# A fused gated-scan and FFN layer on eight cores: one of two calls of a LayerNorm phase is taken out of the block loop

## What is computed

```python
x = x + attn(layernorm(x))      # layer A
x = x + ffn(layernorm(x))       # layer B
# attn: h = rmsnorm(x); q,k,v,g = h @ wq, h @ wk, h @ wv, h @ wg
#       a = sigmoid(h @ wa); y_t = a_t * y_(t-1) + k_t * v_t   (scan over tokens)
#       return (q * y * silu(g)) @ wo
# ffn:  xr, xk = blends of x and x shifted by one token (mu_r, mu_k)
#       return sigmoid(xr @ W_r.T) * (square(relu(xk @ W_k.T)) @ W_v.T)
```

## Time and profile before

| | us |
|---|---|
| median of 2 runs (lowest, highest) | 871.05 (869.91, 872.19) |
| the profiled execution, own time | 864.63 |
| its span on the slowest core, core 4 | 863.1 |
| spans of all cores | 834.6 to 863.1 |
| PE, DVE, ACT busy on core 4 | 622.9, 350.2, 275.0 |

### The profile page before, as it was taken

One profiled execution on the slowest core, in us unless ns is written; L12 is line 12 of the kernel. 1 busy time (PEld: TensorE's weight loads), 2 busy tenths in 40 slices (PEclk: granted clock), 3 DMA queues, 4 the chain that ended last, 5 costly groups with the idle time before them and its releaser, 6 DMA issues.

```text
span 863.1 us, 12981 instructions; the slowest of 8 cores (834.6 to 863.1 us)
## 1 busy us (share of the span) xinstructions
PE 622.9 (72%) x4864; PEld 522.8 (61%) x4864; DVE 350.2 (41%) x656; ACT 275.0 (32%) x432; POOL 5.1 (1%) x13
## 2 busy tenths in 40 slices
PE   0000008799789799959896999799979697998085
PEld 0000006687678588948795888587858596877064
DVE  0002702323824374437343833383437443834222
ACT  2000003126233614462346134523361435232321
POOL 2000000000000000000000000000000000000000
PEclk9999999988778788979997888788879898888577
DMA  8999992001100410141014101410041003001101
GB/s 168 186 186 165 172 160 37 1 1 26 25 1 12 124 38 1 42 107 26 1 50 102 22 2 49 98 25 1 15 121 38 1 18 82 1 2 49 24 1 49
DMA packets 52876, 48.10 MB, mean 56 GB/s; under 512 B 47440, under 2 KB 47568, under 8 KB 51664
## 3 DMA queue, kind: packets, MB, share of 16 engines
q1 hardware_dynamic: 51520, 28.40, 13.2%
q0 software_dynamic: 1296, 18.87, 13.1%
HBM read 46.22 MB, written 8.39 MB: 63 GB/s over the span
## 4 chain that ended last, share of the span: by engine, by line
PE 53%; DVE 17%; DMA 13%; another core or an unknown queue 7%; ACT 4%; issue 4%; DVEq 1%; SPq 0%; ACTq 0%; POOLq 0%
PE pp L194 50%; DMA xhat_fm<-stg 8%; DVE fC L404 5%; DVE xh_fm L484 3%; PE pp L209 3%; DMA W_wk<-wk 3%; DMA out<-x_tm 2%; DVE y2b L474 2%; DVE fB L395 2%; DMA xh_fm<-bfP 1%; DVE fC L469 1%; DVE x_tm L224 1%; ACT bfP L455 1%; ACT bfP L247 1%
## 5 line engine op out<-in xcount | busy, mean ns | idle before, releaser
L194 PE MATMUL pp<-xhat_fm,W_wk 128*128 128x256 bf16 x512 | 74.7, 321 | 175.3 <-DMA xhat_fm<-stg 175.3
L194 PEld LDWEIGHTS pp<-xhat_fm,W_wk 128*128 128x128 bf16 x512 | 57.9, 114 | 191.3 <-issue 176.6
L194 PE MATMUL pp<-y2b,W_wrT 128*128 128x256 bf16 x512 | 68.8, 305 | 29.9 <-DVE y2b L474 27.4
L194 PE MATMUL pp<-xh_fm,W_wkT 128*128 128x256 bf16 x512 | 71.1, 312 | 19.1 <-DVE fC L414 19.1
L194 PEld LDWEIGHTS pp<-y2b,W_wrT 128*128 128x128 bf16 x512 | 55.5, 109 | 42.1 <-issue 30.5
L194 PEld LDWEIGHTS pp<-xh_fm,W_wkT 128*128 128x128 bf16 x512 | 56.4, 111 | 33.6 <-issue 21.1
L194 PE MATMUL pp<-xhat_fm,W_wg 128*128 128x256 bf16 x512 | 64.7, 294 | 4.4 <-DVE fC L414 4.4
L194 PE MATMUL pp<-xh_fm,W_wvT 128*128 128x256 bf16 x512 | 65.6, 296 | 3.0 <-ACT xh_fm L504 3.0
L194 PE MATMUL pp<-xhat_fm,W_wq 128*128 128x256 bf16 x512 | 64.3, 293 | 1.8 <-ACT fB L386 1.8
L194 PE MATMUL pp<-xhat_fm,W_wv 128*128 128x256 bf16 x512 | 64.3, 293 | 0.0
L194 PE MATMUL pp<-y2b,W_wo 128*128 128x256 bf16 x512 | 64.3, 293 | 0.0
(11 more groups left out here) (64 smaller groups left out, 615.0 us busy)
## 6 DMA issues: line engine op xcount, KB each, us to landing
x_tm<-x SPq DMA_DIRECT2D x16, 512.0 KB, 5.1
out<-x_tm SPq DMA_DIRECT2D x8, 1024.0 KB, 4.4
W_wk<-wk POOLq DMA_DIRECT2D x1, 2048.0 KB, 21.9
W_wv<-wv POOLq DMA_DIRECT2D x1, 2048.0 KB, 35.2
W_wa<-wa POOLq DMA_DIRECT2D x1, 2048.0 KB, 49.1
W_wq<-wq POOLq DMA_DIRECT2D x1, 2048.0 KB, 62.9
W_wg<-wg POOLq DMA_DIRECT2D x1, 2048.0 KB, 76.5
W_wo<-wo POOLq DMA_DIRECT2D x1, 2048.0 KB, 88.5
```

The source lines that it names most:

```text
L194: nc.tensor.matmul(pj[:, h * 256:(h + 1) * 256], wview(wname, kc, douc * 128, (douc + 1) * 128), rhs_fn(kc), start=st, stop=sp)),
```

## The change

`phase_A(b + 2)` stands twice in a pass: right after `phase_E1(b)`, and again at the very end of the pass. Both calls read the same `x_tm` block and write the same values into `stg1`, the statistics and `xhat_fm`. The change deletes the second call.

```diff
@@ the end of the loop over b
         phase_F3(b)
         phase_F4(b)
         phase_G(b)
-        if b + 2 < NB:
-            phase_A(b + 2)
```

## The result

| | before | changed |
|---|---|---|
| median, us (lowest, highest, runs) | 869.19 (858.2, 890.1, 26) | 882.25 (870.92, 902.21, 27) |
| ratio of undisturbed runs | | 1.0122, 95% interval 1.0083 to 1.0162 |
| profiled execution's slowest span, us | 863.1 | 876.0 |

Leaving work out made the kernel 1.2% slower, where 881 us and 1.2% had been forecast. (Some executions of any version show one die much longer at a lower clock; the ratio leaves them out.)

What follows compares the result with a forecast made beforehand. The chain over ScalarE and VectorE from T (residual add) to F2 was taken as the bound, not the wait at k. Adding 6.6 us there and 3.9 for F2's slow starts, called 10, gave 881 us, range 862 to 893.

Steps and rivals of the forecast that it cites:

- The early k: At TensorE's k stage, passes 1 to 6: 41.8 us of waiting only move to q, F1 and F2, buying nothing.
- the bit by which the late, slow k held the copies of line 386: ScalarE's copies of k: the most an earlier k could gain on the path, costed within the T to F2 template.
- The removed work was free: Deleted activations and VectorE work lay under TensorE's W_wvT and wo stages; nothing comes back.
- The table load moved onto the chain: At E1's Sqrt on ScalarE: six table loads of 1.28 us lose their cover and join the chain.
- The step from the earlier trace: ScalarE, T to line 455's shifted copy: 21.62 us with the table load, 20.35 without, difference 1.27.
- The forecast T to F2: From the residual add after TensorE's transposes (T) to stage F2: 46.31 us at reduced clock, 45.98 at full; sum 6.6 including pass 6.
- The slow start of F2 in reduced passes: F2 on TensorE starts slower behind longer idle time: 1.3 us in each of passes 1, 3 and 4, 3.9 in all.
- Pass 6: No phase A left behind E1, line 455 waits for xh2_fm transposes: the load adds its full 1.28 us, T to F2 44.2.
- a price of the deletion that the prediction put at nothing: On queue SP: twelve transposes leave, yet the next pair, for xh2_fm, gains nothing.
- Rival 1: TensorE's wait at k counts in full: 42 us faster, 829 us; chance 0.03.
- rival 4: The Sqrt table load is placed elsewhere, not on the chain: 7.7 us fall away, 873 us; chance 0.06.
- Rivals 2 and 3: TensorE's clock: more of the run reduced, 895 us, chance 0.16; or less of it reduced, 841 us, chance 0.05.

Runs made afterwards that it cites:

- the single Sqrt: Changed kernel plus one 128x2 Sqrt on ScalarE behind the last sigmoid of passes 0 to 5: 841.11 us, ratio 0.9981; second time 841.07, ratio 0.9988.
- the two runs shown above: The changed kernel unaltered on a full-clock chip, 847.58 us, and the changed kernel plus one 128x2 Sqrt in passes 0 to 5, 841.11 us.

## Why the prediction was right, and where its terms were off

**The early k.** It buys nothing while the table load is on the chain: with the transposes put back the time stays at 847.6. The wait of 41.8 us went to q, F1 and F2, as said. With the load under cover it buys a little. Passes 1 to 5 add up to 223.75 us from T to F2 with the single Sqrt, and in the kernel before to 225.63 on core 4 and 226.54 on core 7. The bound of the prediction, "the bit by which the late, slow k held the copies of line 386", is seen in the kernel before in pass 2 of core 7:

```profile
371.58 10.00 PE L194 MATMUL pp<-xhat_fm,W_wk 128*128 128x256 bf16 x64 [9.30 <-DMA xhat_fm<-stg]
```

```profile
360.37:406.51 46.14, 32.87 (x274) 28.02 (x273) 27.35 (x56) 18.71 (x30) 0.00 (x0) 0.87 0.27 58
```

The first row is the k stage in the timeline of TensorE, the second the window from T to F2. The last copy of k waits 1.12 us for that stage, and line 455 starts at T + 21.79 instead of T + 20.35. With the load on the chain line 455 isn't due before T + 21.8, so a late k costs nothing there. In whole kernels the early k and all else that was removed, apart from the table, are worth 842.7 - 841.11 = 1.6 us (second time 1.7, within the interval).

**The removed work was free.** Shown for the statistics by putting them back. For the 12 VectorE operations over 128x1024 it is argued; with the rest they cost 1.6 us at the most.

**The table load moved onto the chain.** Shown by the single Sqrt: 1.29 us in pass 1, and 6.5 us of the changed kernel's 847.58. The step from the earlier trace rows was the right one to read. The forecast T to F2, 45.98 at full clock and 46.31 at the reduced one, measured 45.98 to 46.28 on the chips with full clock and up to 46.63 in a reduced pass.

**The slow start of F2 in reduced passes.** Right in kind, too small in size: 1.3 us a pass was taken from core 4's 9.88. In the changed kernel F2 takes 10.34 to 10.40 behind a wait of 5.6 us, against 8.56 in the earlier trace rows, so 1.8. Together with 1.2 to 1.5 us more from T to F2 (46.34 and 46.63 against 45.11) this is the 3.0 to 3.2 us by which a reduced pass grew. It would also explain why the ratio was 1.0122 with such passes and 1.0054 without; that is argued from the traces, since no run here turned the reduced clock on or off by itself.

**Pass 6.** The term was mis-sized. I forecast 44.2 us; it took 45.93 on core 5, 44.66 on core 7, and 44.80 and 45.28 in the two runs shown above. Line 455 waits there for the `xh2_fm` transposes, and these took longer than in the earlier trace rows: 751.65 - 744.29 = 7.4 us from their issue on core 5. The same distance in pass 6 is 6.3 us on all eight cores in the kernel before, and again with the transposes put back and with F1 done twice. It is 6.4 to 7.6 in the changed kernel and 7.3 to 8.4 with the single Sqrt or the statistics back. So putting the deleted transposes back takes this delay away, a price of the deletion that the prediction put at nothing. But F1 done twice takes it away too, so the cause stays open. It costs up to 2 us once here, and in the version with early copies of k it decides.

**The total.** The forecast share, 1.2%, was met closer than its terms. Between T of pass 0 and T of pass 7 the two profiled executions differ by 16.7 us: 8.6 from T to F2, where 6.6 were forecast, and 8.1 from F2 to T, where 3.9 were. The start and the end, which the change doesn't touch, were 3.8 us shorter in the changed kernel's execution, and the spans differ by 12.9. So the mechanism was right, both terms were too small, and the agreement to a tenth of a percent is in part luck.

**The rivals.** Rival 1 (the wait at k counts) and rival 4 (the load doesn't move) are refuted by the runs. Rivals 2 and 3 hung on the share of reduced clock. The clock of the slowest core was 0.868 against 0.858, so the share on it did not grow; that more cores have such stretches is seen in one profiled execution of each, and isn't settled.

## What to carry to other kernels

The largest wait of an engine may be worth next to nothing, here at most 1.6 of 41.8 us: measure from where the chain forks (here T) to where it joins again (F2), and look for a pass in which the wait is already absent. Before redundant work is taken out, ask what state it leaves behind; here an activation table, whose load then fell onto the chain, and a Sqrt of two columns is enough to keep it. When one engine's queue carries the chain, fill its short waits for other engines with work that stands later in the queue.

## What the runs showed of the hardware

- Useless matmuls can pay: 64 more a pass in a wait of 7 us made the stage behind it 7.15 us instead of 9.5 and the kernel 10 us faster, at unchanged T to F2. A wait of up to 2.25 us left the stage at 7.15 there; one of 3.95 us did not. The length of the wait alone doesn't settle it: behind the wait of 3.0 us for line 504 in pass 7 the last stage took 7.15 us on cores 1, 2, 3 and 7 of the kernel before, and 8.42 and 10.03 on cores 0 and 6, each behind a stage of 7.15.
- In the stretches at the reduced clock a matmul stage has a granted clock of 0.81 and takes 8.4 us instead of 7.0. Windows of one stage each on core 4 of the kernel before:

```profile
257.74:266.14 8.40, 8.40 (x67) 6.96 (x65) 2.98 (x2) 2.39 (x4) 0.00 (x0) 0.81 0.00 0
429.47:436.46 6.99, 6.99 (x66) 6.25 (x64) 3.02 (x3) 2.39 (x4) 0.00 (x0) 1.00 0.01 2
```

- These stretches differ by chip and by core: the profiled executions of the eleven runs on the two chips at 843 us show none, with all 8 cores at work, and within one execution they come by pairs of cores (clocks before: 0.868 and 0.876 on cores 0 and 1, 0.899 on 2 and 3, 0.858 on 4 and 5, 0.925 and 0.924 on 6 and 7). Times of 843 and 869 us for the same kernel go with that.
- A pair of DMA transposes of 128x1024 took 6.3 us from issue to the start of its reader in many places, and up to 8.4 in others.
